# GpSimd's order in a two-layer graph attention kernel: each scaling pass behind the 1/sigma of its own rows, and four residual buffers for two

## The reference

```python
# layer 0, per graph: 8 heads of 32
q, k, v = x @ Wq + bq, x @ Wk + bk, x @ Wv + bv
attn = softmax(where(adj == 0, -inf, q @ k.T / sqrt(32)))
y = (attn @ v) @ Wo + bo + x
x = (y - mean(y)) * rsqrt(var(y) + 1e-5) * gamma + beta
# layer 1, per graph: 8 heads of 32, weights transposed, no 1/sqrt(32), mask value -16384
z = z0 = v
for _ in range(4):
    z = 0.9 * pros @ z + 0.1 * z0
y = x + z
out = (y - mean(y)) / sqrt(var(y) + 1e-5) * gamma + beta
```

## Time and profile before

| | before |
|---|---|
| median of 3 runs | 935.65 us (934.45 to 936.67) |
| the profiled execution | 937.12 us, of which the span from first to last instruction is 935.1 us |
| mean granted clock of TensorE | 0.943 |
| PE busy | 828.2 us (89%) |
| DVE busy | 773.6 us (83%) |
| ACT busy | 659.1 us (70%) |
| POOL busy | 566.2 us (61%) |

### The profile page before, as it was taken

How to read it: one execution, slowest core, us unless ns; L and a number is a source line. 1 busy time by engine, 2 the same in 40 slices (tenths; PEclk the granted TensorE clock), 3 DMA queues, 4 the chain that set the end, 5 groups by cost and what they waited for, 6 DMA issues and landing times. The chain is left out here.

```text
span 935.1 us, 33758 instructions
## 1 busy us (share of the span) xinstructions
PE 828.2 (89%) x11544; PEld 744.4 (80%) x11544; DVE 773.6 (83%) x3376; ACT 659.1 (70%) x2667; POOL 566.2 (61%) x421
## 2 busy tenths in 40 slices
PE   4688999999999999999999999999999999999884
PEld 4577888888888888888888888888888888887762
DVE  4467889989888988989888998888989889888764
ACT  4356887777777777777676777777777777767562
POOL 0125656657666666666666676666666666666664
PEclk9888999999999999999999999999999999999898
DMA  6011110111101111101101111010111011000001
GB/s 201 18 29 30 31 30 25 42 41 42 30 30 42 30 35 42 43 24 37 42 23 42 42 43 30 31 42 24 42 41 42 28 34 41 14 25 13 14 13 35
DMA packets 33222, 34.21 MB, mean 37 GB/s; under 512 B 2336, under 2 KB 28832, under 8 KB 33056
## 3 DMA queue, kind: packets, MB, share of 16 engines
q1 hardware_dynamic: 33056, 32.06, 11.4%
HBM read 23.67 MB, written 8.39 MB: 34 GB/s over the span
## 5 line engine op out<-in xcount | busy, mean ns | idle before, releaser
L586 ACT ACTIVATE ex<-sm,nmax 128x128 f32<-128x128 f32 x1024 | 398.5, 394 | 80.0 <-DVE nmax L736 79.5
L923 POOL TENSOR_TENSOR pr<-ex,rec 128x1024 f32<-128x1024 f32 x128 | 245.1, 1915 | 244.2 <-DVE rec L745 244.2
L736 DVE CUSTOM_DVE_ANT_0 sm<-psS,mask 128x128 f32<-128x128 f32 x1024 | 228.1, 283 | 12.8 <-PE psS L382 10.9
L586 ACT ACTIVATION_READ_ACCUMULATOR ex<-sm,nmax 128x1 f32 x1024 | 197.1, 192 | 0.0
L392 PE MATMUL psF<-ident,pr 128*128 128x128 f32 x1024 | 150.6, 277 | 4.3 <-POOL pr L923 1.4
L333 PE MATMUL psF<-xh,w_hi 128*128 128x256 f32 x512 | 127.0, 334 | 15.6 <-DVE w_lo L677 9.1
L392 PEld LDWEIGHTS psF<-ident,pr 128*128 128x128 f32 x1024 | 114.2, 141 | 19.3 <-issue 9.0
L443 PE MATMUL psF<-ident,hT 128*128 128x128 f32 x512 | 97.6, 295 | 25.7 <-DVE v L725 21.8
L333 PE MATMUL psF<-xh,w_lo 128*128 128x256 f32 x512 | 116.3, 313 | 0.0
L333 PE MATMUL psF<-xl,w_hi 128*128 128x256 f32 x512 | 115.4, 311 | 0.0
L333 PEld LDWEIGHTS psF<-xh,w_hi 128*128 128x128 f32 x512 | 93.9, 226 | 17.3 <-issue 13.2
(11 more groups left out here) (65 smaller groups left out, 1562.4 us busy)
## 6 DMA issues: line engine op xcount, KB each, us to landing
xt_in<-in_x_t SPq DMA_DIRECT2D x32, 256.0 KB, 2.7
x_in<-in_x SPq DMA_DIRECT2D x32, 256.0 KB, 2.9
out<-o_t SPq DMA_DIRECT2D x32, 256.0 KB, 2.2
adj_in<-in_adj SPq DMA_DIRECT2D x32, 128.0 KB, 2.1
w_raw<-in_w SPq DMA_DIRECT2D x7, 256.0 KB, 5.0
row<-in_rows SPq DMA_DIRECT2D x1, 768.0 KB, 6.6
ident<-in_ident SPq DMA_DIRECT2D x1, 64.0 KB, 4.0
col<-in_cols SPq DMA_DIRECT2D x1, 7.0 KB, 4.4
```

The source lines that it names most:

```text
L586: e = nc.scalar.activation(ex[l][:, b, h, :], sm[l][:, b, h, :], ACT.Exp, scale=-1.0, bias=nmax[l][:, b, h:h + 1], accum_out=tot[l][:, b, ...
L736: last = nc.vector.tensor_tensor_reduce(sm[l][:, b, h, :], psS[:, o:o + N], mask[p.parity][:, b, :], -1.0, BIG, ALU.add, ALU.min, nmax[l][ ...
L923: nc.gpsimd.tensor_tensor(pr[l][:, b, :, :], ex[l][:, b, :, :], rec[l][:, b, :].unsqueeze(2).broadcast_to([128, H, N]), ALU.mult).then_inc ...
```

## The change

GpSimd's step is put in another order, and `zf` has four buffers instead of two.

- `scale_out(t - 6)` stands directly behind `inverse_root(1, t - 6)`, ahead of `last_term(t - 4)` and of `inverse_root(0, t - 2)`; before, it stood behind both.
- `scaled_residual` stands directly behind `inverse_root(0, t - 2)` and works on the same pair t-2; before, it stood near the end of the step, behind three probability passes, and worked on pair t-3.
- As the residual is begun a step earlier, its buffer lives longer: it is `zf[p.number % 4]`, and it waits for the hop of pair p-4 and no longer p-2.

```diff
-        zf = [sb(f"zf{i}", [128, 2, D]) for i in range(2)]
+        zf = [sb(f"zf{i}", [128, 2, D]) for i in range(4)]
...
-                        dst, add = y1[p.parity], zf[p.parity]
+                        dst, add = y1[p.parity], zf[p.number % 4]
...
                     for b in range(2):
-                        pool.wait_ge(z_s[NUM_HOP - 1][b].sem, z_s[NUM_HOP - 1][b].at(p - 2))
+                        if p.number >= 4:
+                            pool.wait_ge(z_s[NUM_HOP - 1][b].sem, z_s[NUM_HOP - 1][b].at(p - 4))
...
                 restart_term(t - 4)
                 inverse_root(1, t - 6)
+                scale_out(t - 6)
                 last_term(t - 4)
                 inverse_root(0, t - 2)
-                scale_out(t - 6)
+                scaled_residual(t - 2)
                 probabilities(1, 1, t - 3)
                 probabilities(0, 1, t - 1)
                 probabilities(0, 0, t - 1)
-                scaled_residual(t - 3)
                 add_bias(t - 1)
```

More of the change, by code:

```diff
@@ L949, in scaled_residual @@
                     for b in range(2):
-                        pool.wait_ge(z_s[NUM_HOP - 1][b].sem, z_s[NUM_HOP - 1][b].at(p - 2))
-                    nc.gpsimd.tensor_tensor(zf[p.parity][:, :, :], xn[p.parity][:, :, :], both(row[:, GA0:GA0 + 1, :]),
+                        if p.number >= 4:
+                            pool.wait_ge(z_s[NUM_HOP - 1][b].sem, z_s[NUM_HOP - 1][b].at(p - 4))
+                    nc.gpsimd.tensor_tensor(zf[p.number % 4][:, :, :], xn[p.parity][:, :, :], both(row[:, GA0:GA0 + 1, :]),
                                             ALU.mult).then_inc(xg_s.sem, 1)
                     pool.wait_ge(xg_s.sem, xg_s.at(p))
-                    nc.gpsimd.tensor_tensor(zf[p.parity][:, :, :], zf[p.parity][:, :, :], both(r_row[:, :, :]), ALU.add
+                    nc.gpsimd.tensor_tensor(zf[p.number % 4][:, :, :], zf[p.number % 4][:, :, :], both(r_row[:, :, :]), ALU.add
                                             ).then_inc(xr_s.sem, 1)
@@ L969, in last_term @@
                     pool.wait_ge(xr_s.sem, xr_s.at(p))
-                    nc.gpsimd.tensor_tensor(zf[p.parity][:, :, :], z0s[:, :, :], zf[p.parity][:, :, :], ALU.add
+                    nc.gpsimd.tensor_tensor(zf[p.number % 4][:, :, :], z0s[:, :, :], zf[p.number % 4][:, :, :], ALU.add
                                             ).then_inc(zf_s.sem, 1)
```

## The result

The changed kernel takes 1022.73 us in the median of 4 runs (1019.09 to 1023.65); before takes 935.05 us (933.71 to 936.67, 4 runs). The ratio is 1.093, with a 95% interval of 1.0897 to 1.0962: slower by 9%. The profiled execution took 1019.09 us, with a span of 1017.1 us and a mean granted clock of 0.90.

What follows compares the result with a forecast made beforehand. Bound: a ring of PE and DVE, in which a microsecond between `split_hi` and the end of `xn` is one of the step. Profiled 937.1 us + 71.4 (wait) - 4.7 (early) + 11.8 (clock) = 1015.6; median 1014, range 1000 to 1042.

Steps and rivals of the forecast that it cites:

- The ring: PE and DVE wait on each other; a microsecond added between `split_hi` and the end of `xn` lengthens the step by one.
- The wait, 2.55 us: DVE waits some 4.5 us for layer 0's `rstd`, so `xn` ends 2.55 us later in each of 28 steps.
- xn at 0.73: Both `xn` instructions on DVE take 0.73 us together, from 2.72, as GpSimd has nothing to run beside them.
- The rival in which it stays slow: `xn` on DVE stays at 2.72 us in each step: +60 us, 1075 us; chance 0.03.
- Nothing else moves: Residual, probability passes, `last_term`, buffers and DMA cost nothing; PE's second probability pass keeps 0.7 us of cover.
- The early steps, -4.7 us: At t = 3, 4, 5, without `scale_out`, `xn` is freed of the probability pass: 3 x (2.31 - 0.73).
- The clock, +11.8 us: PE's longer wait for `xn` gives one half-clock stretch every step: 28 x (1.54 - 1.12).
- the signs of being wrong: DVE finds `rstd` ready, `xn` stays at 1.35 us, PE waits for the second probability pass, or clock well under 0.94.
- The rival of two stretches: PE has two half-clock stretches in each step: +43 us, 1057 us; in half the steps 1036; chance 0.17 above 1036.
- The rival "faster": `o_t` passes finish before DVE reaches `xn`, which alone gets shorter by 1.99 us: 871 us at best; chance 0.03.

Runs made afterwards that it cites:

- fill: Overwritten matmuls put ahead of PE's wait for `xn`: 28 in the changed kernel, 980.86 us; 8 in the kernel before, 899.74 us.
- the added wait: Kernel before, with GpSimd waiting for `xn` of pair t-2 before it starts `scale_out`, no work moved: 838.5 us.
- the last experiment: Changed kernel with `scale_out` moved behind the three probability passes, residual place and four buffers kept: 841.6 us.
- the shorter chain: Changed kernel with `last_term` moved from between `scale_out` and layer 0's `rstd` to behind the probability passes: 958.47 us.

## Why the prediction was right

The forecast was 1014 us in a range of 1000 to 1042, slower with 0.95. The measured 1022.73 lies in it, 8.7 above the forecast. The mechanism was right; that the total came so near is in part luck, as the clock term was too small by 13 us and smaller misses partly made up for it. Step by step:

- **The ring.** That a microsecond between `split_hi` and the end of `xn` is one of the step was shown in both directions: with 1.21 us out of the chain the full-clock step is 27.41 us, from 28.70 measured with fill (24.13 + 3.77 + 0.72 = 28.62 by the sum), and 1.99 us out of `xn` brings the step to PE's busy time.
- **The wait, 2.55 us.** Measured 5.74 - 3.24 = 2.50 us. DVE's idle time was forecast at 4.4 us, 125 us in all; it is 4.40, 123.7 us in all. The moved `scale_out` alone makes it, and with `last_term` out of the way it is 1.21 us shorter.
- **xn at 0.73.** Measured 0.73. The rival in which it stays slow has no part in this kernel (its 64 instructions are busy 23.5 us, forecast 26). That GpSimd's passes make it slow was shown from both sides, by the added wait (0.73) and by `scale_out` moved alone (2.30). The rule in the Trainium skill, page SBUF — State Buffer, section Who interferes with whom, that whichever starts first holds the shared ports for its whole instruction, agrees with the trace of `scale_out` moved alone: a pass that starts 0.07 us ahead of `xn` holds it up by 2.30 - 0.73 = 1.57 us. The runs show that a GpSimd pass beside `xn` does this; they do not show that the ports are the way.
- **Nothing else moves.** Right: the residual's move, tried alone, left the steady steps as they were, and in the full steps PE never waited for a probability pass.
- **The early steps, -4.7 us.** From the `xn` of t = 2 to that of t = 5 it is 65.2 us, before 72.8: -7.6 us. Of this 1.8 us can't be put down to the change: the kernel of the last experiment does the same work in the same order there and has 67.0, and the difference lies between t = 2 and t = 3, where its granted clock is 0.85 and the changed kernel's 0.90.
- **The clock, +11.8 us.** This is the term that was mis-sized. I took one half-clock stretch a step at 1.54 us, for 1.12 before; the stretch in a steady step has double length, and the step pays 30.68 - 28.70 = 1.98 us, for 1.07 before. From the `xn` of t = 5 to that of t = 33 it is 853.3 us, before 758.1: +95.1. Less 28 x 2.50 for the wait, 25.1 us remain for the clock, twice the forecast; the filled kernels give the same, 28 x (1.98 - 1.07) = 25.5. Of the signs of being wrong that the prediction names, this one came, a granted clock well under 0.94: it is 0.90, and a step is 30.7 us where I had 30.2 with one stretch. The rival of two stretches had the right mechanism and too high a price, 3.1 us: the first part lies on the end of PE's idle time (568.07 to 568.95 above), and the wait for v shrinks from 0.72 to 0.27 us, since PE comes to it late (line 425 takes 1.09 us there, 0.63 in the earlier trace rows).
- **The rival "faster".** It had small chance and did not come, but its bound was wrong: with the added wait the time is 838.5 us, under the 871 that I held to be the most. I let PE gain only its wait for `xn` and the clock, 34 + 31 = 65 us. In the 28 steps it gained 85.2, as the wait for v went too (28 x 0.72 = 20 us).

The span sums up: +95.1 in the full steps, -7.6 early, -3.3 before the first `xn` and -2.3 behind the last: +82 us, from 935.1 to 1017.1. The parts before the first and behind the last `xn` are differences of single executions (that first `xn` comes between 44.7 and 49.1 us in all kernels here), and I read no cause from them. The medians differ by 87.7 us; the other 5.7 are the place of the two profiled executions, 3.6 below the median after and 2.1 above it before. In the forecast of the span, +78.5, the clock was 13.3 too low, and against it stand 1.4 for the wait, 2.9 early and 5.6 at both ends.

## What to carry to other kernels

When a pass is put directly behind what it needs, look at what stands behind it in the same engine's order: a pass that waits for another engine holds up every later result of its own engine, and here the first engine wanted one of them. Where an instruction takes a multiple of the time that its twin of the same shape takes, look at what GpSimd or VectorE runs beside it before believing that it is slow; a wait on an engine with idle time can be worth 10%. An idle stretch of TensorE has a second price in its clock (here 1.07 to 1.98 us a step). Give it bounds from the rows and not a fixed sum.

## What was not expected of the hardware

The mean price of the half clock in a step does not grow evenly with the wait ahead of it. With PE waiting 1.23 us for `xn` it was 1.07 us a step, with 2.5 us it was 1.02, and with 3.7 us it was 1.98. With 5.3 us (`scale_out` alone) a step is 31.74 us in the mean of 25, which leaves about 1.5 over the 30.3 that I estimate at full clock (28.70 + 1.57). In the changed kernel the steady steps from the third to the last but two are 30.6 to 30.95 us; with the shorter chain they vary from 27.4 to 30.3. What makes one step fall to half clock and the next not is left open: these runs vary the length of the wait and fill it, but not its place.
